# GNN layers and MoE on one core: high and low parts of gathered rows made for two edge tiles by one op each

## The reference

```python
def _sage_layer(x, src, dst, Wl, bl, Wr, a):
    msg = x[src]
    agg = segment_sum(msg, dst, num_segments=n)
    deg = segment_sum(ones, dst, num_segments=n)
    agg = agg / maximum(deg, 1.0)[:, None]
    out = agg @ Wl + bl + x @ Wr
    return where(out >= 0, out, a * out)

x = x + three_sage_layers(layernorm(x))
...
x = x + moe(layernorm(x))
```

## Time and profile before

| what | value |
| --- | --- |
| median of 3 runs | 2687.99 us (2687.64 to 2690.53) |
| the profiled execution's own time | 2686.95 us |
| its span, first to last instruction | 2685.2 us |
| mean granted TensorE clock | 0.994 of full |
| gather stages, from the first `highs` to the last | 344.4 us to 1892.9 us, three of them |
| TensorE, VectorE, ScalarE, POOL busy | 98%, 67%, 47%, 37% of the span |

### The profile page before, as it was taken

One profiled execution on the slowest core, in us unless ns is written; L12 is line 12 of the kernel. 1 busy time (PEld: TensorE's weight loads), 2 busy tenths in 40 slices (PEclk: granted clock), 3 DMA queues, 4 the chain that ended last, 5 costly groups with the idle time before them and its releaser, 6 DMA issues.

```text
span 2685.2 us, 39728 instructions
## 1 busy us (share of the span) xinstructions
PE 2625.3 (98%) x9195; PEld 1506.2 (56%) x9195; DVE 1805.6 (67%) x5090; ACT 1272.2 (47%) x2681; POOL 990.5 (37%) x1054
## 2 busy tenths in 40 slices
PE   7999999999999999999999999999899999999999
PEld 3444445554688855555588855555455555555554
DVE  5555555554899955555699955555477777777775
ACT  2222245554588855555388855555122222222222
POOL 2222255553344445554233335555122222222221
PEclk9999999999999999999999999999999999999999
DMA  4444378887355568887355558888422222222221
GB/s 133 133 133 133 118 224 270 266 271 229 100 164 164 164 214 263 274 263 257 97 164 165 164 181 273 263 274 263 145 78 82 82 86 90 82 82 85 87 85 48
DMA packets 200943, 446.57 MB, mean 166 GB/s; under 512 B 34383, under 2 KB 34695, under 8 KB 200836
## 3 DMA queue, kind: packets, MB, share of 16 engines
q0 software_dynamic: 64928, 207.55, 27.2%
q10 hardware_dynamic: 69168, 126.12, 12.9%
q1 hardware_dynamic: 66740, 111.54, 11.9%
HBM read 238.50 MB, written 207.11 MB: 166 GB/s over the span
## 4 chain that ended last, share of the span: by engine, by line
PE 94%; DMA 2%; DVE 2%; ACT 1%; issue 1%; SPq 0%; POOL 0%; DVEq 0%; POOLq 0%; ACTq 0%
PE psY L590 11%; PE psH L570 10%; PE psY L570 10%; PE psM L698 9%; PE psY L698 9%; PE psH L698 8%; PE psT L564 6%; PE psY L604 5%; PE psY L612 5%; PE psY L621 5%; PE psS L710 4%; PE psS L711 4%; PE psM L570 2%; PE psH L590 1%; PE psS L564 1%; PE psH L799 1%
## 5 line engine op out<-in xcount | busy, mean ns | idle before, releaser
L498 POOL DMA_INDIRECT rows<-y_rows,lists x471 | 485.4, 1031 | 475.7 <-PE psS L711 355.0
L1175 DVE TENSOR_TENSOR lows<-rows,highs 128x512 fp32r<-128x512 f32 x471 | 326.2, 693 | 374.1 <-ACT highs L832 366.6
L505 POOL DMA_INDIRECT rows<-sum_rows,nodeI x237 | 296.0, 1249 | 329.7 <-DVE rows L1183 295.7
L832 ACT ACTIVATE outs<-psS 128x512 f32<-128x512 f32 x471 | 279.8, 594 | 284.5 <-PE psS L711 284.0
L832 ACT ACTIVATE highs<-rows 128x512 fp32r<-128x512 f32 x471 | 294.8, 626 | 143.5 <-ACT outs L832 109.7
L710 PE MATMUL psS<-highs,sel 128*128 128x512 f32 x471 | 348.7, 740 | 7.2 <-ACT outs L832 7.2
L479 POOL TENSOR_TENSOR st<-st,small 128x1 f32<-128x1 f32 x158 | 89.9, 569 | 664.1 <-DVE st L1075 664.1
L590 PE MATMUL psY<-wy,res 128*128 128x512 f32 x632 | 286.6, 596 | 0.7 <-ACT res L832 0.7
L570 PE MATMUL psY<-wy,xTs 128*128 128x512 f32 x632 | 285.2, 594 | 0.0
L570 PE MATMUL psH<-wz,hTs 128*128 128x512 f32 x632 | 284.2, 592 | 0.7 <-ACT hTs L832 0.7
L698 PE MATMUL psM<-wz,res 128*128 128x512 f32 x544 | 255.5, 592 | 0.0
(11 more groups left out here) (166 smaller groups left out, 4109.7 us busy)
## 6 DMA issues: line engine op xcount, KB each, us to landing
sum_rows<-outs ACTq DMA_DIRECT2D x471, 256.0 KB, 3.7
y_rows<-outs SPq DMA_DIRECT2D x237, 256.0 KB, 2.0
rows<-in_x POOLq DMA_DIRECT2D x78, 256.0 KB, 2.9
outs<-in_x SPq DMA_DIRECT2D x78, 256.0 KB, 2.6
out_rows<-res SPq DMA_DIRECT2D x78, 256.0 KB, 2.0
rows<-y_rows,lists POOLq DMA_INDIRECT x471, 4.2
rows<-sum_rows,nodeI POOLq DMA_INDIRECT x237, 3.5
wy<-in_L_gnn_Wl SPq DMA_DIRECT2D x3, 1024.0 KB, 7.3
```

The lines of the kernel that those rows point to most:

```text
L498: pool.indirect_dma_start(out=rows[:, t % RING, :], out_offset=None, in_=y_d, in_offset=bass.IndirectOffsetOnAxis(ap=col(srcT, t), axis=0) ...
L505: pool.indirect_dma_start(out=rows[:, s, :], out_offset=None, in_=s_d, in_offset=bass.IndirectOffsetOnAxis(ap=col(nodeI, t), axis=0), boun ...
L832: act.activation(o, i_, ACT.Copy).then_inc(signal, 1)
L1175: dve.tensor_tensor(lows[:, t % RING, :], rows[:, t % RING, :], highs[:, g, :].bitcast(F32), ALU.subtract)\
```

## The change

One op makes the high parts of a pair of tiles, and one op their low parts. `doubled(p)` gives for pair p (tiles 2p and 2p+1) the first slot in `highs`, the first in `rows`, and the number of tiles (the last pair has one). `hi_set` and `lo_set` have two members instead of four, one for even and one for odd pairs, raised once a pair. ScalarE makes pair b+1 ahead of both copies of block b; VectorE makes both selection matrices first, then the low parts of the pair. TensorE, POOL and SyncE issue the same instructions in the same order, TensorE with the new counts in its waits. Line numbers after line 333 move by some lines: 710 and 711 become 716 and 717, 698 becomes 703, 832 becomes 838, 1175 becomes 1179, 1164 becomes 1168.

```diff
@@ -229,8 +229,8 @@
         oh_set = sems("oh_set", 4)
         oh_used = sems("oh_used", 4)
         edge_in = sems("edge_in", RING)
-        hi_set = sems("hi_set", 4)
-        lo_set = sems("lo_set", 4)
+        hi_set = sems("hi_set", 2)
+        lo_set = sems("lo_set", 2)
         sel_set = sems("sel_set", 4)
         seg_ps = sems("seg_ps", 4)
         seg_sb = sems("seg_sb", 4)
@@ -331,6 +331,11 @@
                 n = P // 4 if b == 0 else uses(g)
                 eng.wait_ge(seg_st[g], 16 * (l * uses(g) + n))
 
+        def doubled(p):
+
+            t = 2 * p
+            return t % 4, t % RING, min(2, ET - t)
+
         def two_on(edges):
 
             return [(i, c + 2) for i, c in edges if not (isinstance(i, int) and 4 * i + c + 2 >= ET)]
@@ -705,8 +710,9 @@
                 before = (g + 2) % 4
                 pe.wait_ge(seg_sb[before], l * uses(before) + n + (g >= 2))
                 pe.wait_ge(sel_set[g], used + 1)
-                pe.wait_ge(hi_set[g], used + 1)
-                pe.wait_ge(lo_set[g], used + 1)
+                p = t // 2
+                pe.wait_ge(hi_set[p % 2], l * uses(p % 2) + p // 2 + 1)
+                pe.wait_ge(lo_set[p % 2], l * uses(p % 2) + p // 2 + 1)
                 pe.matmul(psS[g % 2][:, :], sel[:, g, :], highs[:, g, :], start=True, stop=False)
                 pe.matmul(psS[g % 2][:, :], sel[:, g, :], lows[:, t % RING, :], start=False, stop=True)\
                   .then_inc(seg_ps[g], 1)
@@ -855,12 +861,12 @@
                 act.wait_ge(y_st[s], 16 * (k * uses(s) + n))
                 copy(outs[:, s, :], psY[s][:, :], y_sb[s])
 
-            def high(i, c, l):
-                t, g, n = at(i, c, 4)
-
-                act.wait_ge(edge_in[t % RING], landed(t, l))
-                act.wait_ge(seg_ps[g], l * uses(g) + n)
-                copy(highs[:, g, :], rows[:, t % RING, :], hi_set[g])
+            def high(p, l):
+                g, r, w = doubled(p)
+                for k in range(w):
+                    act.wait_ge(edge_in[r + k], landed(2 * p + k, l))
+                    act.wait_ge(seg_ps[g + k], l * uses(g + k) + p // 2)
+                copy(highs[:, g:g + w, :], rows[:, r:r + w, :], hi_set[p % 2])
 
             def take_sums(i, c, l):
                 t, g, n = at(i, c, 4)
@@ -915,14 +921,12 @@
 
                 all_turns(act, y_ps, l + 1)
                 all_turns(act, y_st, l + 1, 16)
-                high(0, 0, l)
-                high(0, 1, l)
-
-                for nodes, edges in sum_blocks():
-                    ahead = two_on(edges)
-                    for k, e in enumerate(edges):
-                        for a in ahead[k:k + 1]:
-                            high(*a, l)
+                high(0, l)
+
+                for b, (nodes, edges) in enumerate(sum_blocks()):
+                    if b + 1 < NT:
+                        high(b + 1, l)
+                    for e in edges:
                         take_sums(*e, l)
                     for e in edges:
                         store_sums(*e, l)
@@ -1169,11 +1173,11 @@
                 dve.tensor_scalar(sel[:, g, :], iota[:, :], col(headT, t), None, ALU.is_equal)\
                    .then_inc(sel_set[g], 1)
 
-            def low(i, c, l):
-                t, g, n = at(i, c, 4)
-                dve.wait_ge(hi_set[g], l * uses(g) + n + 1)
-                dve.tensor_tensor(lows[:, t % RING, :], rows[:, t % RING, :], highs[:, g, :].bitcast(F32), ALU.subtract)\
-                   .then_inc(lo_set[g], 1)
+            def low(p, l):
+                g, r, w = doubled(p)
+                dve.wait_ge(hi_set[p % 2], l * uses(p % 2) + p // 2 + 1)
+                dve.tensor_tensor(lows[:, r:r + w, :], rows[:, r:r + w, :], highs[:, g:g + w, :].bitcast(F32),
+                                  ALU.subtract).then_inc(lo_set[p % 2], 1)
 
             def next_x(i, c, k):
 
@@ -1357,19 +1361,18 @@
                 if l == 0:
                     make_plan()
                 dve.wait_ge(bvec_in, 16 * (l + 1))
-                def take_edge(e):
-                    select(*e, l)
-                    low(*e, l)
-
                 take_z(0, 0, l)
                 take_z(0, 1, l)
-                take_edge((0, 0))
-                take_edge((0, 1))
+                select(0, 0, l)
+                select(0, 1, l)
+                low(0, l)
                 for t in range(2, FIRST):
                     take_z(t // 2, t % 2, l)
-                for nodes, edges in sum_blocks():
+                for b, (nodes, edges) in enumerate(sum_blocks()):
                     for e in two_on(edges):
-                        take_edge(e)
+                        select(*e, l)
+                    if b + 1 < NT:
+                        low(b + 1, l)
                     for node in nodes:
                         take_z(*node, l)
```

## The result

| what | before | with the change |
| --- | --- | --- |
| median of 4 runs | 2689.23 us (2687.64 to 2690.53) | 2715.22 us (2713.74 to 2716.87) |
| the profiled execution's own time | 2686.95 | 2716.87 |
| span, mean granted clock | 2685.2, 0.994 | 2715.2, 0.994 |

The ratio is 1.0097, 95% interval 1.008 to 1.0115: 26 us slower, forecast 20, range 2700 to 2721.

A forecast was written before the change was run, and what follows sets the result against it. TensorE was taken to set the pace in the gather stages; 33 places losing 0.61 us each add 20.1 us to 2686.95 or the median 2687.99, giving 2707.6 us between the two sums, range 2700 to 2721.

The forecast's parts named there:

- What bounds the kernel: Gather stages: TensorE sets the pace, busy 99.13 of 100 us; ScalarE and VectorE run ahead of it.
- 33 places: First tile behind each block without a node, 11 a layer in 3 layers, block 0 not counted: 20.1 us lost together.
- Prices of the wide ops: Ops of 1024 columns: high part on ScalarE 1.06 us, low part on VectorE 1.227 us.
- the price of two whole ops: Upper bound, a wide op costing two narrow ones: high 1.258 us, low 1.384; 0.96 us a place, 31.7 in all.
- Ordinary blocks: Blocks of two edge tiles and one node: nothing lost, TensorE's 4.36 us covering the wide ops.
- two gathers: A pair's wide high waits for both tiles' gathers: cost 0, with 2.5 us of cover at the median landing.
- openings: Block 0 of each layer, covered by three whole node products: taken as 0, at most 1.8 us.
- The loss of 0.61 us a place: Behind blocks without a node, tile 80's second matmul comes at 508.69 instead of 508.08; 33 such make 20.1 us.
- Rival 1, ready in time: Both wide ops end early enough at the 33 places, losing 0.10 us each: 2690 us; chance 0.06.
- Rival 2, the saved cost reaches the end: Lighter engines let the copy of `psS` begin 0.5 us earlier at the 33 places: 2670.5 us; chance 0.03.
- the prediction's sign of so much less *busy* time: ScalarE and VectorE would be some 44 and 37 us less busy.
- Rival 3, the clock: Pauses at the 33 places drop TensorE's clock to half, 59 us more: 2766 us; chance 0.03.

## Why the prediction was right, and by what it was short

- *What bounds the kernel*: right. TensorE sets the pace, and all that moved are the 33 places behind blocks without a node.
- *Prices of the wide ops*: right within 0.01 us each. The slope from same-kind rows was the right choice; twice the narrow op would have given 0.96 us a place. That the result lies inside the range is partly luck: the upper end came from the price of two whole ops, which neither trace nor run bears out, and made room for the 7.6 us above the forecast that came from elsewhere.
- *Ordinary blocks, two gathers, openings cost nothing*: right. Not one tile outside the 33 places came later for good; the openings differ by 0.7 us or less in the first layer.
- *The loss of 0.61 us a place*: mis-sized, 0.73 in most places. It took the 0.46 us between copy and high and the 0.39 us of restart from rows whose instructions had fewer waits, or another order of them. With the added waits the wide high began 0.53 us after the copy, 0.07 later; the range named these waits, but gave them no price. And from the release to the second matmul it was 0.46 us in place of 0.39. With one wait fewer and the order turned they were 0.48 and 0.40, and the loss 0.60. In the sum: 33 x 0.12 = 4 us.
- *Left out*: that store issue is not always as quick as in the row I read. Six places lost 0.28 to 1.08 us more, 3.7 us in all. Two of them, as said, had stores of usual length and a high that began late all the same. The trace of before has a slow issue too (1.82 us at 472.99), but it stands ahead of an ordinary block, where even a high 0.87 us late cost nothing; ahead of its 33 places no two stores took over 1.0 us. What a slow one would have cost there, that trace doesn't show; in the run with narrow ops in the new order, stores of 1.12 to 1.25 us cost up to 0.2 us. A typical row gave the sum, and the tail of its group wasn't asked for. The prediction held that the other 32 places repeat the distances of block 39 within some hundredths. One doesn't, and showed what was to come: at block 6 of layer 1 the high began 0.74 us after the copy in place of 0.46, and only the time to spare hid it:

```profile
995.43 0.63 ACT L832 ACTIVATE highs<-rows 128x512 fp32r<-128x512 f32 x1 [0.74 <-ACT outs L832]
```

- *The rest*: of the remaining 1.5 us of the profiled execution 0.7 lie in the first opening; behind it, the part between the second and the third stage got 1.8 us shorter and the part behind the last one 2.8 us longer, which I can't tell from the difference between two executions of one kernel.
- *Rival 1, ready in time*: the wide low took 1.226 us, so no. Its sum has a slip on which nothing hangs: 507.69 less 505.98 is 1.71 us, not 1.68, and the rival's loss 0.07 us a place, not 0.10. *Rival 2, the saved cost reaches the end*: ScalarE's and VectorE's time was saved (45 and 37 us by group, though the prediction's sign of so much less *busy* time came out as 25 and 16), and none of it arrived. *Rival 3, the clock*: 1.00 in the middle of the stage, 0.994 in all, as before.

## What to carry to other kernels

Merging two ops saves a fixed part on an engine, and lengthens the way to the *first* half of the result. Look for the place where the waiting engine is closest behind, not at the average: here 33 of 237 pairs decided. Here the better cure was on the side of the engine that sets the pace: spreading its filler work evenly made wide and narrow ops alike, and gained 10 us that neither version of the ops could.

## What the runs showed of the hardware

- The number of waits ahead of an op, and their order, are seen. ScalarE's high behind two stores began 0.46 us after the copy with two waits, 0.48 with three and 0.53 with four. TensorE's second matmul came 0.46 us after the release by the last of four waits, and 0.40 after one by the first.
- Issue of two stores on ScalarE's queue takes 0.95 us mostly, but up to 2.88 us in the changed kernel (block 22 of layer 0, ahead of an ordinary block, where it cost nothing) and 2.02 us ahead of one of the 33 places, and the compute op behind them in the program waits.
- POOL's gather instructions got longer with the wide low ops: mean 1031 ns before, 1203 with the change. Two of them in the changed kernel, the first beside a wide low that began at 498.80, the second not:

```profile
499.52 1.39 POOL L503 DMA_INDIRECT rows<-y_rows,lists  x1 [1.17 <-PE psS L717]
...
501.71 1.01 POOL L503 DMA_INDIRECT rows<-y_rows,lists  x1 [0.80 <-PE psS L717]
```

With narrow lows in the new order the mean was 1043 ns. The traces show when it happens. In the changed kernel all 185 gathers of over 1.19 us begin while a low is under way, and so do all such gathers in every other run; the 256 that begin at another time take 1.18 us at most, beside other VectorE ops too. A gather that begins inside a low, more than 0.05 us after its start and with 0.2 us or more of it to go, ends 0.88 to 0.90 us after the low's end, in every run: in the first row above the low ends at 500.03 and the gather at 500.91. So a longer low catches more gathers, and holds each for longer. POOL has idle time between gathers, so nothing came of it here. The Trainium skill (SBUF — State Buffer, SBUF: two separate sides) tells of a port pair that VectorE and GpSimd share, where whoever starts first keeps it for a whole instruction; it counts in a VectorE op with two SBUF inputs, but only against a GpSimd op that reads SBUF. The low has two SBUF inputs, and these rows would fit; whether the gather's issue is such an op, no run isolated.
